# Fourier-layer kernel: column-tiled forward transforms, squares with the channel innermost, a new order on four engines, and the weights' sign on ScalarE

## The chip, the cores and the metric

The kernel runs on one core of a Trainium2 chip. The metric is the device time of one execution in microseconds (us); lower is better. Five compute queues matter: TensorE (PE in the rows, with its weight loads as PEld), VectorE (DVE), ScalarE (ACT), GpSimd (POOL) and SyncE (SP), which only issues transfers.

## The reference, cut to what matters

64 images of 64x64 pixels go through a Fourier neural operator with 32 channels and 4 layers; its tokens, and 77 text tokens, then go through one attention block and one layer of experts.

```python
def spectral_conv(x, w1, w2):                       # x: image, channel, 64, 64
    x_ft = jnp.fft.rfft2(x)
    out_ft[:, :, :M1, :M2]  = einsum('bixy,ioxy->boxy', x_ft[:, :, :M1, :M2], w1)   # M1 = M2 = 12
    out_ft[:, :, -M1:, :M2] = einsum('bixy,ioxy->boxy', x_ft[:, :, -M1:, :M2], w2)
    return jnp.fft.irfft2(out_ft)
h = layer_norm(x @ fc0_w + fc0_b)                   # over the 32 channels
for i in range(4):
    h = layer_norm(spectral_conv(h) + conv_w[i] @ h + conv_b[i])
    if i < 3: h = gelu(h)
h = gelu(h @ fc1) ; h = gelu(h @ fc2) ; h = h @ fc3
```

All numbers are fp32.

## The kernel before, in words

**Passes.** Images are taken in 32 pairs (`PAIRS`). A first pass (the stem) computes the first layer norm in closed form and the forward transform of each pair. Three layer passes follow (`layer(s)`, s = 1, 2, 3), each over the 32 pairs, then a last pass with the three dense layers, then attention and experts. Between passes `mix(s)` multiplies the modes of all images by the layer's weights. The change lies almost wholly in the three layer passes, at about 277 to 765, 800 to 1280 and 1316 to 1800 us.

**One step of a layer pass** handles pair g and finishes pairs g-1 and g-2. A pair is worked in halves h (0, 1) of 1024 values per partition, and each half in units u (0, 1) of 128x512. On TensorE the operations of a step are:

- `widen` (line 527): the inverse transform along x, 512 columns, into the bank that becomes the layer's output; `conv` (line 544) adds the 1x1 convolution on top of it and releases the bank to ScalarE.
- `i1` (line 555): the inverse transform along y for the next pair, 64 products of 32 columns, read out by `z_copy` on ScalarE and VectorE.
- `turn` (line 591): four transposes of the pair before into the single bank `t_mid`, which `hc_copy` (ScalarE, line 929) must empty before the next `turn` may write it. Four `turn`s a step.
- `f1` (line 615): the forward transform along x of the pair before. Per step 128 products, each with 128x32 weights taken from the activations `hp` and 48 moving columns `d1`, in four groups of 32 products; each goes to one of four column tiles 32 wide. A channel takes two products per column tile pair (`a`), and each writes real and imaginary parts interleaved. `a_copy` (ScalarE, line 945) empties the single bank `a_ps` after each group.
- `f2` (line 629): the forward transform along y of pair g-2, two groups of 12 products with 128x64 weights from `asb` and 24 moving columns, on two column tiles 64 wide; `x_copy` reads it out.

An fp32 product is two records in the profile, so a group of 32 products shows as x64; a transpose is one.

**The layer norm** goes round four engines for each unit: `square` (ScalarE, line 903) writes the squares to `sq`, `reduce` (VectorE, line 1238) sums 33 numbers per pixel, `rstds` (POOL, line 1481) takes the power -0.5, `normalise`, `gain` and `bias` (VectorE, lines 1252, 1309, 1316) apply it, and `gelu` (ScalarE, line 915) writes `hp`. `sq` stands as [channel, pixel], 33 x 16, so a pixel's numbers are 16 apart. A bank is used again by `widen` once `normalise` has read it.

**Weights.** Every second step SyncE loads one chunk of the next layer's weights (`load_w`), `w_sum` (VectorE, line 1346) sums it, and `w_centre` (POOL, lines 1491 to 1497) subtracts the mean and multiplies one half by the signs `sgn`; `load_w` of the next chunk waits for that.

**Order.** Nothing is scheduled by a program: each engine runs its queue in the order in which the functions are called, and waits by semaphores. SyncE's queue in a step is `load_w` (every second step), `load_h` for half 0, `store_h` of pair g-2 half 1, `store_h` of pair g-1 half 0 (after both of its `hc_copy`), `load_h` for half 1, and six loads of `gin`, the coefficients of pair g+2, which ScalarE's `coefficients` (lines 967, 969) put in order.

## Time and profile before

| | |
|---|---|
| median of 3 runs | 3216.27 us (3214.8 to 3220.66) |
| profiled execution | 3222.97 us, of which the span is 3221.1 us |
| mean granted TensorE clock | 0.965 of full speed |
| busy share of the span | TensorE 90%, VectorE 69%, ScalarE 67%, POOL 65% |

The rows below come from the profiled execution. Busy shares are means over passes with different limits, so the layer passes are read by themselves. A group's duration reaches a little into the next group of the same engine, so the advance from one group to the next is the difference of their starts.

### The profile page before, as it was taken

To read this page: it belongs to the slowest core of one execution; us is meant where nothing else is said; L and a number is where in the kernel's file an instruction comes from. 1 tells how busy PE (TensorE), PEld (TensorE's weight loads), DVE (VectorE), ACT (ScalarE), POOL (GpSimd) and SP (SyncE) were. 2 spreads that over 40 slices of the span, in tenths; PEclk is the share of its full clock that TensorE was granted. 3 is DMA by queue.
4 is the path that set the end of the run, shared out by engine and by line. 5 is a ranking of instruction groups with operands and counts; after the bars stand their busy time and mean duration, and the time that the engine had idled before them with its cause. 6 is when DMAs were issued, how large, how long until landed. Compare 5 with 4: busy or idle time off the path is not lost. (4 is left out here: it accounts for less than half of the span.)

```text
span 3221.1 us, 190782 instructions
## 1 busy us (share of the span) xinstructions
PE 2893.1 (90%) x80542; PEld 1961.7 (61%) x80542; DVE 2215.7 (69%) x3767; ACT 2148.5 (67%) x3644; POOL 2102.1 (65%) x1147
## 2 busy tenths in 40 slices
PE   6777999997999999699999689999999987999997
PEld 4555777775677777477777534444444424666665
DVE  7765889884888887488898444444444436777775
ACT  4663777774677776477777257777777764666654
POOL 3763899993899997499999344445445434666664
PEclk9997999998899999899999889999999998999998
DMA  5764555554455554455555411111211103111111
GB/s 164 229 224 142 172 173 176 181 172 142 148 176 179 171 181 143 146 175 174 177 175 179 137 52 53 58 55 58 58 55 58 58 21 79 31 30 30 30 30 24
DMA packets 236925, 379.78 MB, mean 118 GB/s; under 512 B 117090, under 2 KB 154786, under 8 KB 236530
## 3 DMA queue, kind: packets, MB, share of 16 engines
q1 hardware_dynamic: 225122, 363.94, 36.7%
q10 hardware_dynamic: 7920, 10.03, 1.0%
q0 software_dynamic: 3744, 3.84, 0.8%
q8 instruction: 101, 1.65, 0.2%
q14 instruction: 38, 0.31, 0.0%
HBM read 217.88 MB, written 159.83 MB: 117 GB/s over the span
## 5 line engine op out<-in xcount | busy, mean ns | idle before, releaser
L1481 POOL TENSOR_TENSOR rstd<-var,mhalf 128x16 f32<-128x16 f32 x512 | 1524.3, 2993 | 694.3 <-DVE var L1238 688.8
L1238 DVE TENSOR_REDUCE var<-sq 128x16 f32<-128x528 f32 x384 | 403.3, 1051 | 93.0 <-ACT sq L903 93.0
L1252 DVE TENSOR_TENSOR zt<-ps,rstd 128x512 f32<-128x512 f32 x512 | 345.1, 684 | 77.8 <-POOL rstd L1481 71.4
L615 PEld LDWEIGHTS ps<-d,hp 128*32 128x32 f32 x24576 | 292.0, 111 | 132.2 <-ACT hp L915 97.3
L615 PE MATMUL ps<-d,hp 128*32 128x48 f32 x24576 | 345.0, 209 | 27.2 <-ACT hp L915 15.2
L544 PEld LDWEIGHTS ps<-cwl,hc 64*64 64x64 f32 x16384 | 272.3, 139 | 139.6 <-issue 133.5
L527 PE MATMUL ps<-zb,ex 48*128 48x512 f32 x1024 | 305.0, 672 | 51.2 <-DVE zt L1252 20.5
L555 PEld LDWEIGHTS ps<-dyi,gt 64*48 64x48 f32 x16384 | 230.1, 124 | 164.2 <-issue 152.5
L1074 ACT ACTIVATE a<-ps,fc1b 128x1024 f32<-128x1024 f32 x256 | 271.1, 1110 | 64.8 <-PE ps L818 64.8
L544 PE MATMUL ps<-cwl,hc 64*64 64x64 f32 x16384 | 308.2, 226 | 0.0
L903 ACT ACTIVATE sq<-ps 128x512 f32<-128x512 f32 x384 | 218.9, 598 | 132.9 <-PE ps L544 123.8
L555 PE MATMUL ps<-dyi,gt 64*48 64x32 f32 x16384 | 272.4, 210 | 36.5 <-ACT gt L969 16.5
L945 ACT COPY asb<-ps 128x384 f32<-128x384 f32 x384 | 191.2, 498 | 169.5 <-PE ps L615 169.5
L1238 DVE TENSOR_REDUCE var<-sql 128x16 f32<-128x528 f32 x128 | 141.6, 1108 | 208.1 <-ACT sql L903 208.1
L915 ACT ACTIVATE hp<-zt 128x512 f32<-128x512 f32 x384 | 231.8, 627 | 78.9 <-DVE zt L1316 78.9
L1309 DVE TENSOR_TENSOR zt<-zt,gbx 128x512 f32<-128x512 f32 x384 | 275.4, 717 | 10.2
L591 PE MATMUL ps<-ident,hp 128*128 128x128 f32 x1536 | 275.5, 303 | 6.3 <-ACT ho L929 4.3
L1316 DVE TENSOR_TENSOR zt<-zt,gbx 128x512 f32<-128x512 f32 x384 | 264.7, 689 | 10.3
L834 PE MATMUL ps<-a,fc 128*64 128x512 f32 x1024 | 253.8, 616 | 3.5 <-ACT a L1074 3.5
L2136 POOL TENSOR_TENSOR sm<-sm,mx 128x952 f32<-128x952 f32 x96 | 170.5, 1776 | 94.7 <-DVE mx L2047 94.7
L929 ACT COPY ho<-ps 128x512 f32<-128x512 f32 x384 | 223.2, 581 | 13.1 <-PE ps L591 5.1
L591 PEld LDWEIGHTS ps<-ident,hp 128*128 128x128 f32 x1536 | 203.5, 197 | 28.9 <-ACT ho L929 7.8
(199 smaller groups left out, 4800.6 us busy)
## 6 DMA issues: line engine op xcount, KB each, us to landing
h_scratch<-ho SPq DMA_DIRECT2D x256, 512.0 KB
hc<-h_scratch SPq DMA_DIRECT2D x256, 512.0 KB, 4.2
wsb<-in_w SPq DMA_DIRECT2D x64, 288.0 KB
gin<-g_scratch SPq DMA_DIRECT2D x252, 72.0 KB
gin<-g_scratch SPq DMA_DIRECT2D x504, 36.0 KB
wc<-expert_scratch SPq DMA_DIRECT2D x64, 129.0 KB, 2.7
g_scratch<-hp ACTq DMA_DIRECT2D x32, 192.0 KB, 4.5
g_scratch<-hp SPq DMA_DIRECT2D x32, 192.0 KB, 4.1
```

The source lines that it names most:

```text
L527: nc.tensor.matmul(main_ps(s, h, u), ex[k], zb[b][k, h, :], start=True, stop=False, skip_group_check=True, tile_position=(64 * u, 0))
L544: last = nc.tensor.matmul(main_ps(s, h, u)[64 * m:64 * m + 64, r:512:8], hc[b][k, 8 * h + r, 64 * m:64 * m + 64], cwl[k], start=False, sto ...
L555: last = nc.tensor.matmul(z[c][64 * u:64 * u + 2 * TRIG, 32 * col:32 * col + 32], gt[b][rows, k].rearrange("k n s a -> k (n s a)"), dyi[ro ...
L591: last = nc.tensor.transpose(t_mid[:, 128 * a:128 * a + 128], src, ident[:])
L615: last = nc.tensor.matmul(a_ps[row:row + 32, 2 * TRIG * k:2 * TRIG * k + 2 * TRIG], hp[b][:, u, 8 * j + k].rearrange("p v r -> p (v r)"), ...
L834: last = nc.tensor.matmul(f2_ps[64 * v:64 * v + 64, u, :], fc2[:], a1[:, 2 * u + v, :], start=True, stop=True, tile_position=(0, 64 * v))
L1074: nc.scalar.activation(a1[:, 2 * u:2 * u + 2, :], f1_ps[:, 2 * u:2 * u + 2, :], ACT.Gelu, bias=fc1b[:]).then_inc(a1_ready, 1)
L1238: nc.vector.tensor_reduce(dst, src, axis=AX.X, op=ALU.add).then_inc(var_ready, 1)
L1252: nc.vector.tensor_tensor(by_px(zt[h][:, u]), by_px(main_ps(s, h, u)), scale, ALU.mult).then_inc(norm_ready, 1)
L1309: nc.vector.tensor_tensor(z, z, channels(s, 0).unsqueeze(2).to_broadcast([128, C, 16]), ALU.mult).then_inc(gain_ready, 1)
L1316: nc.vector.tensor_tensor(z, z, channels(s, 1).unsqueeze(2).to_broadcast([128, C, 16]), ALU.add).then_inc(zt_ready, 1)
L1481: nc.gpsimd.tensor_tensor(rstd[u][:], var[u][:], mhalf[:], ALU.pow).then_inc(rstd_ready, 1)
```

## The change

- **`f1`** takes each half of the trigonometric matrix by itself: a product now has 24 moving columns (`dx`) in place of 48, one column tile pair holds the real and one the imaginary parts, and one group covers 16 channels (64 products) in place of 8, with the same 128 products per step. `a_copy` then runs twice a step in place of four times, as a plain copy of 128x384. `asb` is one buffer [channel, x mode] in place of two.
- **`f2`** uses four column tiles 32 wide: 24 products per group in place of 12, with 128x32 weights that are read 24 elements apart, and `dy` as moving operand.
- **`square`** reads its bank 16 elements apart and writes `sq` as [pixel, channel], so `reduce` reads contiguously.
- **The sign** of the weights is applied by ScalarE (`w_sign`, in the odd half step of every second pair) in place of POOL, except in the first pass; `w_centre` moves between two powers of the second pair, and `w_sum` from the end to the start of the first pair's step.
- **Orders**: TensorE runs `conv`, `i1` in one piece, `f1`, `turn`, `f1` where `f1` and `i1` alternated; ScalarE's and VectorE's queues are reordered; SyncE's queue is as before. Weights and constants are laid out for this, and two constants more are loaded.

```diff
             def f1(s, b, g, j):
...
-                pe.wait_ge(a_ready, 4 * rank(s, g) + j)
-                for k in range(8):
-                    for a in range(2):
+                pe.wait_ge(a_ready, 2 * rank(s, g) + j)
+                for k in range(CH):
+                    for part in range(2):
                         for u in range(2):
-                            row = 64 * a + 32 * u
-                            last = nc.tensor.matmul(a_ps[row:row + 32, 2 * TRIG * k:2 * TRIG * k + 2 * TRIG],
-                                                    hp[b][:, u, 8 * j + k].rearrange("p v r -> p (v r)"),
-                                                    d1[:, a].rearrange("p x s -> p (x s)"),
+                            row = 64 * part + 32 * u
+                            last = nc.tensor.matmul(a_ps[row:row + 32, 2 * KX * k:2 * KX * k + 2 * KX],
+                                                    hp[b][:, u, CH * j + k].rearrange("p v r -> p (v r)"), dx[:, part],
                                                     start=True, stop=True, tile_position=(0, row))
...
                 for a in range(6):
                     for c in range(2):
-                        o = KY * (6 * m + a)
-                        last = nc.tensor.matmul(x_ps[64 * c:64 * c + 64, o:o + KY],
-                                                asb[b][:, KX * m + 2 * a + c].rearrange("y c s -> y (c s)"),
-                                                cy[:], start=True, stop=True, tile_position=(0, 64 * c))
+                        for part in range(2):
+                            o, row = KY * (6 * m + a), 64 * c + 32 * part
+                            last = nc.tensor.matmul(x_ps[row:row + 32, o:o + KY], asb[:, :, KX * m + 2 * a + c],
+                                                    dy[:, part], start=True, stop=True, tile_position=(0, row))
...
                     if here:
                         widen(s, 0, g, 1)
+                        conv(s, 0, g, 1)
+                        with where_next(g):
+                            i1(s, g + 1, 0, CH)
                     if old:
                         f1(s, 0, g - 1, 0)
-                    if here:
-                        conv(s, 0, g, 1)
-                    for j, piece in enumerate(((0, 6), (6, 11), (11, 16))):
...
+                    if old:
+                        turn(s, 0, g - 1, 1, 0)
+                        f1(s, 0, g - 1, 1)
...
-                    dst = sq[u][:, 0:C, :].rearrange("p (v c) n -> p v (c n)", v=2)
...
+                    dst = sq[u][:, :, 0:C]
+                by_px = (lambda tile: tile.rearrange("p (v n) -> p v n", v=2)) if is_last(s) else (
+                    lambda tile: tile.rearrange("p (c n) -> p n c", c=C))
+                nc.scalar.activation(dst, by_px(main_ps(s, h, u)), ACT.Square).then_inc(sq_ready, 1)
...
-                nc.scalar.copy(asb[b][:, :, 8 * j:8 * j + 8, :].rearrange("p x g s -> p g x s"),
-                               a_ps.rearrange("p (g x s) -> p g x s", g=8, s=2)).then_inc(a_ready, 1)
+            def a_copy(s, g, j):
+
+                act.wait_ge(a_psr, 2 * rank(s, g) + j + 1)
+                nc.scalar.copy(asb[:, CH * j:CH * j + CH].rearrange("p c x -> p (c x)"), a_ps).then_inc(a_ready, 1)
...
+            def w_sign(s, i):
+
+                k = COUPLES * s + i
+                first = wsb[:, bass.ds(i * WCH, WCH), 0, :]
+                act.wait_ge(w_sub, 2 * k + 2)
+                nc.scalar.activation(first, first, ACT.Copy, scale=sgn[:]).then_inc(w_cent, 1)
...
                 def odd(i, p):
                     here, old, nxt = (where(i, p, 0, lag) for lag in (0, 2, -2))
-                    if old:
-                        a_copy(s, 0, old[0], 0)
                     if here:
                         square(s, here[0], 1, 0)
+                    if old:
+                        hc_copy(s, old[0], 0, 1)
+                        a_copy(s, old[0], 0)
+                    if here:
                         square(s, here[0], 1, 1)
-                    if old:
-                        a_copy(s, 0, old[0], 1)
-                        a_copy(s, 0, old[0], 2)
                     if nxt:
                         z_copy(s, nxt[0])
                     if old:
                         hc_copy(s, old[0], 1, 0)
-                        a_copy(s, 0, old[0], 3)
+                        a_copy(s, old[0], 1)
+                    if here and p == 1:
+                        w_sign(s, i)
...
                 else:
-                    dst, src = var[u][:], sq[u][:].rearrange("p c n -> p n c")
+                    dst, src = var[u][:], sq[u][:]
                 nc.vector.tensor_reduce(dst, src, axis=AX.X, op=ALU.add).then_inc(var_ready, 1)
...
                                         ALU.subtract).then_inc(w_sub, 1)
+                if s is not STEM:
+                    return
...
                         for u in range(2):
                             rstds(s, 2 * i + p, h, u)
-                        if p == 0 and h == 1 and not final:
-                            w_centre(s, i)
+                            if p == 1 and h == 0 and u == 0 and not final:
+                                w_centre(s, i)
```

TensorE's queue before, in the middle of a layer step, from `widen` of half 1 on (`d` is `d1`; x counts products):

```order
L527 MATMUL ps<-zb,ex 128x512 x2
L608 REGISTER_ALU
L615 MATMUL ps<-d,hp 32x48 x32
L544 MATMUL ps<-cwl,hc 64x64 x32
L722 COMPARE_AND_BRANCH
L563 ISA
L565 REGISTER_ALU
L555 MATMUL ps<-dyi,gt 48x32 x24
L757 UNCONDITIONAL_BRANCH
L615 MATMUL ps<-d,hp 32x48 x32
L722 COMPARE_AND_BRANCH
L555 MATMUL ps<-dyi,gt 48x32 x20
```

The same stretch of TensorE's queue after the change:

```order
L521 ISA
L530 MATMUL ps<-zb,ex 128x512 x2
L547 MATMUL ps<-cwl,hc 64x64 x32
L724 COMPARE_AND_BRANCH
L566 ISA
L568 REGISTER_ALU
L558 MATMUL ps<-dyi,gt 48x32 x64
L754 UNCONDITIONAL_BRANCH
L611 REGISTER_ALU
L613 REGISTER_ALU
L618 MATMUL ps<-dx,hp 32x24 x64
L594 MATMUL ps<-ident,hp 128x128 x4
```

The first `f1` group no longer stands between `widen` and `conv`, `i1` is one group of 64 products ahead of `f1`, and `turn` (line 594 now) stands between the two `f1` groups.

ScalarE's queue before, from `hc_copy` of half 0 (`ho0`) to the first `a_copy` (`asb0`), with buffer numbers:

```order
L929 COPY ho0<-ps 128x512
L964 ISA
L967 COPY gt0<-gin 128x64x6
L914 REGISTER_ALU
L915 ACTIVATE hp0<-zt1 128x64x8
L922 REGISTER_ALU
L929 COPY ho0<-ps 128x512
L954 REGISTER_ALU
L959 ISA
L959 COPY xsb<-ps 128x144x2
L969 ACTIVATE gt0<-gin,side 128x64x6
L945 COPY asb0<-ps 128x8x24x2
```

ScalarE's queue after the change, from the last `gelu` of the even half step through the odd one:

```order
L914 ACTIVATE hp0<-zt1 128x64x8
L894 REGISTER_ALU
L48 ISA
L903 ACTIVATE sq0<-ps 128x16x32
L921 REGISTER_ALU
L928 COPY ho0<-ps 128x512
L944 COPY asb<-ps 128x384
L903 ACTIVATE sq1<-ps 128x16x32
L948 COPY zb0<-ps 112x16x2x16
L921 REGISTER_ALU
L928 COPY ho1<-ps 128x512
L944 COPY asb<-ps 128x384
```

The second `hc_copy` of half 0 has moved behind the first square of half 1 (`sq0`), and the second square (`sq1`) now stands behind `a_copy`, which waits for an `f1` group of 64 products.

POOL's queue before, from the last power of the first pair of two:

```order
L1481 TENSOR_TENSOR rstd<-var,mhalf 128x16
L1489 ISA
L1491 TENSOR_SCALAR wmean<-wmean 128x18
L1492 ISA
L1493 ISA
L1493 TENSOR_TENSOR wsb<-wsb,wmean 128x576
L1495 REGISTER_ALU
L1497 TENSOR_TENSOR wsb<-wsb,sgn 128x9x32
L1479 ISA
L1481 TENSOR_TENSOR rstd<-var,mhalf 128x16
```

POOL's queue after the change, from the first power of the second pair:

```order
L1490 TENSOR_TENSOR rstd<-var,mhalf 128x16
L1498 ISA
L1500 TENSOR_SCALAR wmean<-wmean 128x18
L1501 ISA
L1502 ISA
L1502 TENSOR_TENSOR wsb<-wsb,wmean 128x576
L1488 REGISTER_ALU
L1490 TENSOR_TENSOR rstd<-var,mhalf 128x16
```

The multiplication by `sgn` has left POOL's queue (it is ScalarE's `w_sign` now), and the other two instructions stand one power later.

## Rows read from the trace of the kernel before

**Rows 1.** Busy time by engine in 380 us in the middle of the second layer.
```profile
880.00:1260.00 380.00, 367.17 (x15290) 292.00 (x15286) 340.11 (x461) 285.69 (x527) 345.49 (x148) 1.00 0.56 174
```

**Rows 2.** TensorE's timeline, second layer: start, duration, group, records, [idle before].
```profile
1000.57 0.89 PE L615 MATMUL ps<-d,hp 128*32 128x48 f32 x64 [0.31 <-ACT hp L915]
...
1007.96 1.13 PE L527 MATMUL ps<-zb,ex 48*128 48x512 f32 x4 [0.25 <-DVE zb L1321]
...
1010.13 0.71 PE L591 MATMUL ps<-ident,hp 128*128 128x128 f32 x4
1010.77 0.89 PE L629 MATMUL ps<-cy,asb 128*64 128x24 f32 x24
1011.61 0.69 PE L591 MATMUL ps<-ident,hp 128*128 128x128 f32 x4
...
1016.89 0.74 PE L555 MATMUL ps<-dyi,gt 64*48 64x32 f32 x48
1017.56 0.89 PE L615 MATMUL ps<-d,hp 128*32 128x48 f32 x64
1018.38 0.65 PE L555 MATMUL ps<-dyi,gt 64*48 64x32 f32 x40
```

**Rows 3.** POOL's timeline over two image pairs, second layer.
```profile
1005.22 6.04 POOL L1481 TENSOR_TENSOR rstd<-var,mhalf 128x16 f32<-128x16 f32 x2 [0.43 <-DVE var L1238]
...
1024.89 0.27 POOL L1491 TENSOR_SCALAR wmean<-wmean 128x18 f32<-128x18 f32 x1
1025.37 1.16 POOL L1493 TENSOR_TENSOR wsb<-wsb,wmean 128x576 f32 x1 [0.20 <-POOL wmean L1491]
1026.72 0.67 POOL L1497 TENSOR_TENSOR wsb<-wsb,sgn 128x288 f32 x1 [0.19 <-POOL wsb L1493]
...
1034.03 6.03 POOL L1481 TENSOR_TENSOR rstd<-var,mhalf 128x16 f32<-128x16 f32 x2 [0.43 <-DVE var L1238]
```

**Rows 4.** TensorE's timeline in the first pass: the small transform `f2_x`.
```profile
156.77 0.66 PE L678 MATMUL ps<-cy,hp 128*8 128x24 f32 x48
157.35 0.49 PE L512 MATMUL ps<-quad,xin 128*128 128x128 f32 x2
```

**Rows 5.** Groups by line: busy us, mean ns of one, idle before.
```profile
L1238 DVE TENSOR_REDUCE var<-sq 128x16 f32<-128x528 f32 x384 | 403.3, 1051 | 93.0 <-ACT sq L903 93.0
L903 ACT ACTIVATE sq<-ps 128x512 f32<-128x512 f32 x384 | 218.9, 598 | 132.9 <-PE ps L544 123.8
L959 ACT COPY xsb<-ps 128x288 f32 (+1 forms) x96 | 41.4, 432 | 2.8 <-PE ps L629 2.8
L1346 DVE TENSOR_REDUCE wmean<-wsb 128x18 f32 (+1 forms) x64 | 47.8, 748 | 12.3 <-DMA wsb<-in_w 12.2
L1058 ACT COPY hp<-ps 128x384 f32<-128x384 f32 x32 | 15.1, 478 | 28.5 <-PE ps L797 21.2 <-issue 3.6 <-DVE hp L1442 1.6
```

**Rows 6.** ScalarE's timeline: the copy of the transposed half.
```profile
1014.72 0.57 ACT L929 COPY ho<-ps 128x512 f32<-128x512 f32 x1
```

**Rows 7.** SyncE's DMA issues in one step of the second layer.
```profile
1011.71 4.16 SPq L379 DMA_DIRECT2D h_scratch<-ho  x2
1017.12 0.35 SPq L382 DMA_DIRECT2D hc<-h_scratch  x1
...
1019.81 0.72 SPq L308 DMA_DIRECT2D gin<-g_scratch  x2
```

**Rows 8.** ScalarE and its queue before the second layer: rows loaded, then read.
```profile
790.35 0.85 ACTq L308 DMA_DIRECT2D gin<-g_scratch  x2
793.43 0.83 ACT L967 COPY gt<-gin 128x384 f32<-128x384 f32 x1 [9.41 <-DMA gin<-g_scratch]
```

**Rows 9.** First pass: one weight chunk's load, and the sum that reads it.
```profile
107.53 0.37 SPq L369 DMA_DIRECT2D wsb<-in_w  x1
...
111.88 0.75 DVE L1346 TENSOR_REDUCE wmean<-wsb 128x18 f32 x1 [0.73 <-DMA wsb<-in_w]
```

More of the change, by code:

```diff
@@ L109, in token_network @@
         gt = [sb(f"gt{p}", [128, CH, 4, 2, KX // 2]) for p in range(2)]
-        asb = [sb(f"asb{p}", [128, 2 * KX, C, 2]) for p in range(2)]
-        sq = [sb(f"sq{u}", [128, C + 1, 16]) for u in range(2)]
+        asb = sb("asb", [128, C, 2 * KX])
+        grow = sb("grow", [128, 2 * 768])
+        sq = [sb(f"sq{u}", [128, 16, C + 1]) for u in range(2)]
         sql = [sb(f"sql{u}", [128, 2, C + 1, 8]) for u in range(2)]
@@ L1017, in even @@
                         hc_copy(s, older[0], 1, 1)
-                    if here:
-                        square(s, here[0], 0, 1)
-                    if old:
-                        gelu(s, old[0], 1, 0)
-                        hc_copy(s, old[0], 0, 0)
                     if here and nxt:
@@ L1377, in even @@
                     if old:
+                        gain(s, *old, 0)
+                        bias(s, *old, 0)
                         normalise(s, *old, 1)
+                    if here and p == 0:
+                        w_sum(s, i)
+                    if old:
                         gain(s, *old, 1)
-                        bias(s, *old, 1)
                     if here:
                         reduce(s, *here, 1)
+                    if old:
+                        bias(s, *old, 1)
                 def odd(i, p):
@@ L1388, in odd @@
                         gain(s, *old, 0)
-                        bias(s, *old, 0)
                     if here:
                         reduce(s, *here, 0)
+                    if old:
+                        bias(s, *old, 0)
+                    if nxt := where(i, p, 0, -2):
+                        z_copy(s, nxt[0])
                     if old:
@@ L1397, in odd @@
                         gain(s, *old, 1)
-                    if nxt := where(i, p, 0, -2):
-                        z_copy(s, nxt[0])
-                    if old:
                         bias(s, *old, 1)
-                    if here and p == 0:
-                        w_sum(s, i)
                 each_step(dve, lambda i, p, h: odd(i, p) if h else even(i, p), 2, 2)
@@ L2271, in layouts @@
     out["d1"] = d1.reshape(128, 2, TRIG, 2)
+    out["dx"] = d1[:, :, 0].reshape(128, TRIG, 2).transpose(0, 2, 1)
     ex = ex.reshape(2, KX // 2, 2, 2, 128).transpose(0, 2, 3, 1, 4).reshape(2 * TRIG, 128)
```

75 lines of the change are left out of this document (35 added, 40 removed).

## Prediction

> **What bounds the kernel now.** I read the busy time of each engine by stretches first. In the middle of a layer pass TensorE is busy 367 of 380 us (97%), POOL 345 (91%), VectorE 340 (90%), ScalarE 286 (75%), at full clock [rows 1]. So the layer passes hang on TensorE, with POOL and VectorE close behind, and an edit that relieves one of the three alone stops at the next. POOL's timeline gives the length of a step: the same power starts at 1005.22 and at 1034.03 us, two pairs later, so a step takes 14.41 us [rows 3]; 96 steps are 1383 us. Of these 14.41, POOL's four powers take 2 x 6.04 = 12.08, its work on the weights (0.27 + 0.20 + 1.16 + 0.19 + 0.67 = 2.49 every second step) 1.25, and the rest, 1.08, is waiting for VectorE's sums, 0.43 of it in each row shown [rows 3].
>
> TensorE's timeline shows groups without gaps but two: 0.25 before `widen`, which waits for `z_copy`, and 0.31 before the first `f1` group, for `gelu` [rows 2]. A gap like the first stands in every step, one like the second in about every other.
>
> **`f1` and `i1`.** A group of 64 `f1` records advances the queue by 0.82 (1017.56 to 1018.38), or 12.8 ns each. `i1` with 48 records advances by 0.67, one with 40 (0.65 less the overlap of 0.07) by 0.58: so a record costs 11 ns and a group 0.13 of its own [rows 2]. Moving columns halve in `f1`, records stay 256 per step. The nearest row for 24 columns on four column tiles is the stem's `f2_x`: 48 records in 0.58 (156.77 to 157.35) [rows 4], hardly less each than 48 columns cost. Less 0.13 that is 9.4 ns, so a group of 128 takes 128 x 9.4 + 130 = 1.33 us at the least, 1.55 at a full 12.1 ns, and 1.64 if nothing is gained. I take 1.40, since the groups are long: 2 x (1.64 - 1.40) = 0.48 saved per step. `i1` in one piece: 128 x 11 + 130 = 1.54, against 0.67 + 0.58 + 0.58 = 1.83 for three; I take 1.60, 0.23 saved.
>
> **`f2`.** A group advances by 0.84 now (1010.77 to 1011.61), 35 ns for each of 24 records [rows 2]. The new one has 48 records of the shape of [rows 4], so 0.58; the weights read 24 elements apart may cost more. But little of this 0.26 arrives. Three `turn`s stand round the two `f2` groups and share one bank: 0.71 for the transposes [rows 2], 0.57 for ScalarE's copy [rows 6] and two hand-overs of about 0.07 make 1.42 from one `turn` to the next, against 0.64 + 0.84 = 1.48 now. Saved: 2 x 0.06 = 0.12, and TensorE gets two new gaps of 0.2. By the same rule `f2` may cost 0.78 without losing anything of the sum.
>
> **Gaps.** `i1` ends about 3.4 us before `widen` (two `f1` groups and a `turn` follow it) and no longer one `f1` group before, so the 0.25 goes; `f1` now stands behind `conv` and `i1`, so the half of 0.31 goes too. The second `f1` group waits for `a_copy`: 0.48 [rows 5] and the hand-overs against a `turn` of 0.64 between; 0.05. TensorE's step: 14.41 - 0.48 - 0.23 - 0.12 - 0.25 - 0.15 + 0.05 = 13.23.
>
> **Sums and sign.** `reduce` takes 1051 ns for 528 numbers that it reads 16 apart, `w_sum` 748 for 576 side by side [rows 5]; 748 x 528 / 576 = 686, with its fixed part some 700. Four times 0.35 is 1.4 us of VectorE's step, which falls from 12.9 to 11.5. The Trainium skill (SBUF — State Buffer, the note on cachelines in "Door 1: The DMA port swizzle") says that SBUF is read in lines of 16 bytes and that each new line costs; the two rows agree. POOL loses the sign, 0.67 + 0.19, less one hand-over: 2.49 becomes about 1.73, its step without waits 12.08 + 0.87 = 12.95. ScalarE takes the sign: nearest is `x_copy`, 288 numbers in 432 ns [rows 5], 0.25 per step with a factor read beside; it loses two of four `a_copy`, 1.0. It has 25% to spare. So TensorE still sets the step, 0.3 above POOL.
>
> **Squares.** ScalarE now reads the bank 64 bytes apart; no row has that shape. `x_copy` reads 144 elements apart: 432 ns for 288, where 384 contiguous take 478 and 512 take 598 [rows 5], so about 400 by their slope: 30 ns lost. The other bound is VectorE's loss in SBUF, 1051 - 700 over 528 numbers, which gives 340 ns for a square. I take 0.05 per square (0.63 to 0.65), since the reader and the memory are those of `x_copy`, and ScalarE's room hides most of it.
>
> **Moved waits.** The second square of half 1 stands behind `a_copy`, hence behind `i1` and 64 products of `f1`: 1.6 + 1.4 + 0.5 after `conv`. POOL has the power of unit 0 (3.02) meanwhile, begun some 1.4 after `conv`, and is free at 4.4 to 4.5; the second sum is there at about 3.5 + 0.6 + 0.7 + 0.2 = 5.0 if POOL runs close behind. This may cost 0.5 in POOL, which has 13.23 - 12.95 = 0.3 to give and runs behind mostly.
>
> SyncE's queue is unchanged but waits elsewhere. `store_h` of half 0 waits for the `hc_copy` that moved behind a square of half 1, and `load_h` and all six `gin` loads are queued behind it. Now the store is issued well before `load_h` (1011.71 + 4.16 against 1017.12), and the last `gin` load begins 3.05 us after `load_h` (1019.81 + 0.36) [rows 7]. After: `conv` end + 0.1 + 0.5 + 0.6 + 0.1 for square and copy (up to 0.6 more behind `gelu`) + 0.7 for the store + 3.05 = 5.1 to 5.7. `coefficients` of the next step wants them 1.3 after the next first `conv`: 1.6 + 1.4 + 0.64 + 1.4 + 1.06 + 1.12 + 1.3 = 8.5. So 2.8 to 3.4 us are left to land. Alone, the last load (issued at about 790.8) was read at 793.43, 2.6 us later [rows 8]; a chunk of 288 KB in the busy first pass took 4.35 (107.53 to 111.88) [rows 9]. I take 0.1 per step.
>
> The weights: `w_sign` ends about 1.15 before the end of `conv` of half 0, `w_sum` starts 3.4 after it, so the chunk has 4.5 us against 4.35 [rows 9]. Whatever is late falls on VectorE every second step, with `gain` and `reduce` behind it; 0 to 0.25, taken 0.05.
>
> **Sum.** 13.23 + 0.17 = 13.4 us a step; (14.41 - 13.4) x 96 = 97 us less. Two more constants are loaded at the start and three small VectorE instructions added: +2. The profiled execution took 3222.97 us, 6.7 above the median of the runs, so 3128 in its terms and **3121 us** as a median. Its own range, 13.2 to 13.6 a step, is 3102 to 3140.
>
> **The rivals.**
> - *TensorE gains more* (0.15). If an `f1` record falls with its columns, to 6.4 ns, its groups take 0.95 and POOL becomes the bound at 12.95 and a small wait, 13.05: 131 us less, 3087. For it: both `i1` (32 columns, 11 ns) and `f1` (48, 12.8) cost in the order of their columns. Against: 24 columns at 12.1 [rows 4].
> - *Strided squares* (0.10). With 340 ns more per square the chain from `conv` to the power is longer by that in each half: 13.75, 3155. The Trainium skill (PSUM — Partial Sum Buffer, Specifications) gives PSUM lines of 8 bytes and warns of non-contiguous access for matmuls; for ScalarE's reads `x_copy` speaks against it.
> - *The loads are late* (0.10). If `gin` takes 4.35 to land, ScalarE stands in front of `coefficients` for 1 us or more, with the `hc_copy` behind it that `turn` needs, and the step grows until the load fits: about 13.95, 3174.
> - *Slower* (0.05). `f2` costs 35 ns per record now, `f1` 12.8 with twice the columns. If that price belongs to the record and its source and not to weights 64 wide on two tiles, 48 records take 1.68, the turn chain hides nothing, and the step is 13.35 + 2 x 0.84 = 15.0: 60 us more, 3278. It decides from 1.37 us a group, 28 ns a record. The Trainium skill (TensorE: Matmul & The Clock Gate, "Wait — 56ns, not 53.3ns?") speaks for this side: starts never come closer than about 25 ns however few the columns. By that 96 records would be 2.4 us a step in place of 1.2. The trace disagrees already, with 12.1 and 12.8 ns per record on four tiles [rows 2, 4].
> - *Within 0.2%* (0.03): several of these together.
>
> **How the numbers follow.** A measurement tells about 0.2%, 6 us. My forecast has 0.57. The three other faster cases end between 3087 and 3174; leaving out a little at their ends and the last two gives 3085 to 3172 for 8 in 10. Faster by over 0.2%: 0.57 + 0.15 + 0.10 + 0.10 = 0.92; within: 0.03; slower: 0.05.
>
> **What would show it.** Two steps of POOL at 26.8 in place of 28.8 us; `f1` groups of 128 records advancing by 1.40 and `f2` by 0.58, with a gap before the second and third `turn` for the `hc_copy`; no gap before `widen` of half 0; `reduce` at 0.70; squares at 0.63; POOL's waits down to 0.4 a step; `coefficients` rarely waiting for a transfer. I am wrong if a square takes over 0.8, if `coefficients` or `w_sum` wait for DMA in most steps, or if `f1`'s group is below 1.2 or above 1.6.

## The result, and the profile after

The changed kernel takes 3179.16 us (median of 4 runs, 3172.68 to 3184.09), against 3217.68 for the kernel before on the same chip: ratio 0.988, interval 0.986 to 0.990. That is 38.5 us less; 97 were forecast. It is faster, as forecast, but the time lies 7 us above the top of the range. The profiled execution took 3178.70 us. Of all executions of the runs below one, of e9, was in a slower state of the chip (4144 us at a mean granted clock of 0.55, the others of e9 about 3171) and is left out.

First the busy time in 360 us in the middle of the second layer (columns as in [rows 1]: stretch, TensorE, its weight loads, VectorE, ScalarE, POOL, clock, DMA share, GB/s):

```profile
880.00:1240.00 360.00, 339.34 (x16233) 275.30 (x16226) 297.97 (x454) 258.79 (x477) 342.08 (x131) 1.00 0.59 178
```

TensorE is down from 97 to 94%, VectorE from 90 to 83, ScalarE from 75 to 72. POOL is up from 91 to 95%. No engine is full, so something else sets the step. TensorE's timeline (start, duration, group, records, [idle before]) answers to [rows 2]:

```profile
1000.91 1.16 PE L547 MATMUL ps<-cwl,hc 64*64 64x64 f32 x64
...
1002.67 0.97 PE L632 MATMUL ps<-dy,asb 128*32 128x24 f32 x48
1003.57 0.72 PE L594 MATMUL ps<-ident,hp 128*128 128x128 f32 x4
...
1005.49 0.71 PE L594 MATMUL ps<-ident,hp 128*128 128x128 f32 x4 [0.29 <-ACT ho L928]
...
1008.40 1.64 PE L558 MATMUL ps<-dyi,gt 64*48 64x32 f32 x128
1009.97 1.28 PE L618 MATMUL ps<-dx,hp 128*32 128x24 f32 x128
1011.18 0.72 PE L594 MATMUL ps<-ident,hp 128*128 128x128 f32 x4
...
1013.67 1.13 PE L530 MATMUL ps<-zb,ex 48*128 48x512 f32 x4 [0.31 <-issue]
...
1019.97 0.71 PE L594 MATMUL ps<-ident,hp 128*128 128x128 f32 x4 [0.95 <-ACT ho L928]
...
1028.95 1.16 PE L547 MATMUL ps<-cwl,hc 64*64 64x64 f32 x64
```

These two steps take 28.04 us, from 1000.91 to 1028.95, so each of them takes 14.02 in place of 14.41. But the steps of this kernel come out unequal, mostly 13.2 to 14.5 us each, and two of them don't give the mean. POOL's division of a weights' mean stands once in every second step, and the two rows below are 26 steps apart:

```profile
869.02 0.56 POOL L1500 TENSOR_SCALAR wmean<-wmean 128x18 f32<-128x18 f32 x1
...
1230.47 0.56 POOL L1500 TENSOR_SCALAR wmean<-wmean 128x18 f32<-128x18 f32 x1
```

That is 361.45 / 26 = 13.90 in the second layer; the same reading gives 13.86 and 13.87 in the other two, so a step takes **13.88** on average. In the kernel before it gives 14.41 in all three. Of 0.53 x 96 = 51 us, 38.5 arrive as a gain of the whole; the rest is taken up in the last part.

In the rows above, `i1` advances the queue by 1.57 (1008.40 to 1009.97), `f1` by 1.21, `f2` by 0.90. The third `turn` of each step waits for `ho`, that is for `hc_copy`: 0.29 in one step, 0.95 in the next, 0.62 on average. ScalarE's timeline says why that copy is late:

```profile
1002.77 0.59 ACT L928 COPY ho<-ps 128x512 f32<-128x512 f32 x1
1004.05 0.90 ACT L965 COPY gt<-gin 128x384 f32<-128x384 f32 x1 [0.68 <-DMA gin<-g_scratch]
1004.86 0.58 ACT L928 COPY ho<-ps 128x512 f32<-128x512 f32 x1
...
1016.59 0.59 ACT L928 COPY ho<-ps 128x512 f32<-128x512 f32 x1
1018.57 0.86 ACT L965 COPY gt<-gin 128x384 f32<-128x384 f32 x1 [1.39 <-DMA gin<-g_scratch]
```

`coefficients` (L965) stands ahead of it and waits for a transfer. By the list of waits it does so 86 times, for 90.6 us in all; before, the same wait was 26.1 us in 3 places, at the starts of the layers. The loads it waits for are late on SyncE, whose issues answer to [rows 7]:

```profile
1000.07 0.33 SPq L311 DMA_DIRECT2D gin<-g_scratch  x1
...
1003.63 6.63 SPq L382 DMA_DIRECT2D h_scratch<-ho  x2
1010.60 0.35 SPq L385 DMA_DIRECT2D hc<-h_scratch  x1
...
1013.38 0.72 SPq L311 DMA_DIRECT2D gin<-g_scratch  x2
```

The second store of the pair waits for the moved `hc_copy`, which ends at 1009.57, and `load_h` and the six `gin` loads come behind it. `coefficients` waits for all six. The last `gin` load begins at 1013.38 + 0.36 = 1013.74 and is read at 1018.57, 4.8 us later; in the step before, 1000.07 to 1004.05, it was 4.0.

POOL, as in [rows 3], is second:

```profile
1003.72 3.28 POOL L1490 TENSOR_TENSOR rstd<-var,mhalf 128x16 f32<-128x16 f32 x1 [0.80 <-DVE var L1245]
1007.08 0.56 POOL L1500 TENSOR_SCALAR wmean<-wmean 128x18 f32<-128x18 f32 x1
1007.86 1.16 POOL L1502 TENSOR_TENSOR wsb<-wsb,wmean 128x576 f32 x1 [0.22 <-POOL wmean L1500]
1008.97 11.98 POOL L1490 TENSOR_TENSOR rstd<-var,mhalf 128x16 f32<-128x16 f32 x4
```

A single power shown here takes 3.28 us (two took 6.04 before, [rows 3]); `wmean` takes 0.56 in place of 0.27. Last, from the groups by line over the whole run, as in [rows 5], VectorE's sum; it is at the forecast 0.70.

```profile
L1245 DVE TENSOR_REDUCE var<-sq 128x16 f32<-128x528 f32 x384 | 267.9, 698 | 189.5 <-ACT sq L903 173.8
```

Two theories for the missing 0.5 us a step (13.88 in place of 13.4; 0.6 in the two steps shown) follow. **Loads:** the store waits for the moved copy, `gin` lands late, `coefficients` holds up `hc_copy`, and through `turn` and `widen` the delay runs round to the next store. **POOL:** powers and weights, some 13.3 us a step, hold it.

### The profile page after: what moved, and what is told of

It reads as the page before. It is cut to its first block and busy times, and to the rows that moved or that the text cites. A ratio compares the mean times of both kernels' runs of the same rounds, so it can differ in the third digit from the quotient of the medians.

```text
span 3176.9 us, 199484 instructions
## 1 busy us (share of the span) xinstructions
PE 2820.0 (89%) x85132; PEld 1925.4 (61%) x85132; DVE 2086.8 (66%) x3770; ACT 2075.8 (65%) x3500; POOL 2115.6 (67%) x1099
## 5 line engine op out<-in xcount | busy, mean ns | idle before, releaser
L1490 POOL TENSOR_TENSOR rstd<-var,mhalf 128x16 f32<-128x16 f32 x512 | 1554.9, 3057 | 643.9 <-DVE var L1245 643.1
L1245 DVE TENSOR_REDUCE var<-sq 128x16 f32<-128x528 f32 x384 | 267.9, 698 | 189.5 <-ACT sq L903 173.8
L594 PE MATMUL ps<-ident,hp 128*128 128x128 f32 x1536 | 277.1, 304 | 46.7 <-ACT ho L928 41.5
L558 PEld LDWEIGHTS ps<-dyi,gt 64*48 64x48 f32 x16384 | 215.7, 125 | 140.4 <-issue 140.3
L1316 DVE TENSOR_TENSOR zt<-zt,gbx 128x512 f32<-128x512 f32 x384 | 296.5, 772 | 5.6
L618 PE MATMUL ps<-dx,hp 128*32 128x24 f32 x24576 | 271.9, 193 | 31.4 <-issue 29.0
L903 ACT ACTIVATE sq<-ps 128x512 f32<-128x512 f32 x384 | 230.1, 600 | 87.9 <-PE ps L547 86.0
L618 PEld LDWEIGHTS ps<-dx,hp 128*32 128x32 f32 x24576 | 249.7, 110 | 53.2 <-issue 37.8
L914 ACT ACTIVATE hp<-zt 128x512 f32<-128x512 f32 x384 | 240.3, 629 | 59.0 <-DVE zt L1323 53.4
L1323 DVE TENSOR_TENSOR zt<-zt,gbx 128x512 f32<-128x512 f32 x384 | 264.9, 690 | 6.8
L558 PE MATMUL ps<-dyi,gt 64*48 64x32 f32 x16384 | 237.3, 210 | 29.6 <-ACT gt L967 15.9
L944 ACT COPY asb<-ps 128x384 f32<-128x384 f32 x192 | 92.0, 479 | 212.7 <-PE ps L618 212.6
```

What stands on the lines that cost most here:

```text
L558: last = nc.tensor.matmul(z[c][64 * u:64 * u + 2 * TRIG, 32 * col:32 * col + 32], gt[b][rows, k].rearrange("k n s a -> k (n s a)"), dyi[ro ...
L594: last = nc.tensor.transpose(t_mid[:, 128 * a:128 * a + 128], src, ident[:])
L618: last = nc.tensor.matmul(a_ps[row:row + 32, 2 * KX * k:2 * KX * k + 2 * KX], hp[b][:, u, CH * j + k].rearrange("p v r -> p (v r)"), dx[:, ...
L1245: nc.vector.tensor_reduce(dst, src, axis=AX.X, op=ALU.add).then_inc(var_ready, 1)
L1316: nc.vector.tensor_tensor(z, z, channels(s, 0).unsqueeze(2).to_broadcast([128, C, 16]), ALU.mult).then_inc(gain_ready, 1)
L1323: nc.vector.tensor_tensor(z, z, channels(s, 1).unsqueeze(2).to_broadcast([128, C, 16]), ALU.add).then_inc(zt_ready, 1)
```

## The experiments

All times are medians; the ratio is to the kernel before, timed beside each. "After" is the changed kernel. The step is read from rows shown here, or, marked ~, a mean over steps that come out unequal or whose rows are not shown (for the changed kernel that of the three layer passes above).

| kernel | us | ratio (95%) | step |
|---|---|---|---|
| after | 3179 | 0.988 (0.986 to 0.990) | ~13.9 |
| e1: after, store behind the loads | 3131 | 0.973 (0.971 to 0.974) | 13.38 |
| e2: after, half of the powers | 3230 | 1.003 (0.999 to 1.007) | uneven |
| e3: e1 and e2 | 3105 | 0.964 (0.963 to 0.966) | 13.16 |
| e4: after, sign on POOL | 3192 | 0.991 (0.989 to 0.993) | ~14.0 |
| e5: e1, means on VectorE | 3116 | 0.969 (0.968 to 0.971) | 13.18 |
| e6: after, `hc_copy` moved back | 3146 | 0.977 (0.976 to 0.979) | ~13.5 |
| e7: before, store behind the loads | 3219 | 1.001 (1.000 to 1.002) | ~14.4 |
| e8: e1, sign on POOL | 3155 | 0.981 (0.979 to 0.982) | ~13.7 |
| e9: e1, squares strided again | 3171 | 0.985 (0.983 to 0.987) | ~13.8 |
| e10: e3, `f2` weights side by side, copy writes strided | 3119 | 0.970 (0.968 to 0.972) | ~13.4 |
| e11: e1, `gain` short | 3116 | 0.969 (0.967 to 0.971) | ~13.2 |
| e12: e5, `f2` weights as in e10 | 3134 | 0.973 (0.972 to 0.975) | ~13.4 |
| e13: e5, `f2` weights side by side, copy reads strided | **3104** | 0.965 (0.963 to 0.966) | 13.02 |
| e14: e3, `f2` weights as in e13 | 3094 | 0.963 (0.961 to 0.964) | 13.02 |
| e15: after, `coefficients` later | 3144 | 0.978 (0.977 to 0.980) | ~13.5 |

### e1 to e4: loads or POOL

e1, in SyncE's `layer_pass`:

```diff
-                    if h == 0:
-                        for lag in (3, 2):
-                            if c := where(i, p, h, lag):
-                                store_h(s, *c)
+                    if c := where(i, p, h, 3):
+                        store_h(s, *c)
```

> The changed kernel (3179 us, 14.02 us a step), with one edit: in a layer pass SyncE's store of the older row, half 0, which waits for ScalarE's copy in the odd half step, is queued behind the loads of the odd half step and no longer ahead of them. Loads theory: what holds the step at 14.02 and not at 13.4 is that the six loads of gin are issued late (from 1011.3 on, where they could go some 5 us sooner), so that coefficients waits for them 0.7 to 1.4 us in 86 of 96 steps. Then the wait of L965 for a transfer falls from 90 us to under 20, a step takes 13.4 to 13.6, and the time is 3121 to 3140. POOL theory: the step is held by POOL's powers, 3.11 us each beside VectorE, and its weights (13.3 of 14.02 us busy). Then the waits of coefficients go and the step stays within 0.1 of 14.02: 3170 to 3180.

Measured: 3131 us. SyncE's timeline, ScalarE's and POOL's, in that order:

```profile
1011.07 0.33 SPq L385 DMA_DIRECT2D hc<-h_scratch  x1
...
1013.71 0.72 SPq L311 DMA_DIRECT2D gin<-g_scratch  x2
1014.77 0.38 SPq L382 DMA_DIRECT2D h_scratch<-ho  x1
```
```profile
1005.96 0.89 ACT L963 COPY gt<-gin 128x384 f32<-128x384 f32 x1
```
```profile
1006.43 3.28 POOL L1488 TENSOR_TENSOR rstd<-var,mhalf 128x16 f32<-128x16 f32 x1 [0.17 <-DVE var L1243]
...
1033.18 3.27 POOL L1488 TENSOR_TENSOR rstd<-var,mhalf 128x16 f32<-128x16 f32 x1 [0.18 <-DVE var L1243]
```

`coefficients` no longer waits in any step (27.3 us in 3 places are left, the layers' starts). Two steps take 1033.18 - 1006.43 = 26.75, the 26.8 that the prediction named as its sign. The loads theory holds: the place of one store in SyncE's queue is worth 48 us. The edit does two things at once, which it doesn't separate: the last `gin` load is issued 3.4 us after the end of `conv` (1010.70 to 1014.07) in place of 5.4, and the store of half 0 no longer runs ahead of it. POOL is now 98% busy, so it is next.

e2, POOL's power, in the layer passes and the last pass (a constant is set once in the rest):

```diff
-  nc.gpsimd.tensor_tensor(rstd[u][:], var[u][:], mhalf[:], ALU.pow)
+  nc.gpsimd.tensor_tensor(rstd[u][:, 0:8], var[u][:, 0:8], mhalf[:, 0:8], ALU.pow)
```

> The changed kernel, with the powers of the layer passes over 8 of the 16 columns: it leaves out half of the reciprocal deviations (a constant stands there in their place), so POOL's four powers of a step take about half, and POOL's step is some 7.5 us in place of 13.3. POOL theory: the step falls to TensorE's 13.2 to 13.5, 3110 to 3140. Loads theory: coefficients goes on waiting for its transfer in most steps and the time stays at 3165 to 3180.

Measured: 3230 us, *slower* than the changed kernel by 51. POOL is not the bound of the changed kernel, but neither theory had this. TensorE's timeline and the busy times of 5 us in it show part of why:

```profile
436.75 0.97 PE L632 MATMUL ps<-dy,asb 128*32 128x24 f32 x48
439.55 1.12 PE L594 MATMUL ps<-ident,hp 128*128 128x128 f32 x4 [1.83 <-ACT ho L928]
440.60 2.08 PE L530 MATMUL ps<-zb,ex 48*128 48x512 f32 x4
```
```profile
440.00:445.00 5.00, 5.00 (x104) 3.17 (x106) 2.66 (x5) 2.43 (x5) 2.01 (x1) 0.50 0.08 34
```

With POOL quick the step still runs into the late load: `coefficients` waited 2.29 us there, and `turn` 1.83 behind it. Round that idle stretch TensorE's granted clock fell to 0.50 of full, 1.2 in place of 2.4 GHz; `widen` took 2.08 where it takes 1.13 (as again at 450.02). It doesn't do so each time:

```profile
532.37 0.71 PE L594 MATMUL ps<-ident,hp 128*128 128x128 f32 x4 [2.06 <-ACT ho L928]
```

After this longer wait the clock stayed at full (1.00 over 530 to 540 us), and `widen` took 1.13. In the changed kernel the wait of 0.95 in the first rows left the clock at full, but behind one of 1.35, at 1076.16, `conv` took 1.98 where it takes 1.16, at 0.50 over 1078 to 1081 us. So in e2 steps of 13.2 us stand beside steps of 14 to 18. Over the whole run `coefficients` waits 121.5 us for its load in place of 90.6, and TensorE's `turn` 64.8 for the copy in place of 41.5; how the 51 us divide between these waits and the clock, and why the waits are longer with a quicker POOL, no run shows.

e3 joins both edits.

> Both edits together: the store behind the loads and half of the powers left out. If each of the two alone moves little because the other holds the step right behind it, this one alone falls to TensorE's own work, 12.9 to 13.3 a step, 3075 to 3115. Loads theory alone: as with the store behind the loads alone, 3121 to 3140. POOL theory alone: as with half of the powers alone, 3110 to 3140.

Measured: 3105 us. Two of POOL's rows, two steps apart, and 300 us of the first layer pass:

```profile
1009.24 2.01 POOL L1491 TENSOR_TENSOR rstd<-var,mhalf 128x8 f32<-128x8 f32 x1 [2.11 <-DVE var L1243]
...
1035.56 2.02 POOL L1491 TENSOR_TENSOR rstd<-var,mhalf 128x8 f32<-128x8 f32 x1 [2.10 <-DVE var L1243]
```
```profile
370.00:670.00 300.00, 292.77 (x14438) 237.50 (x14440) 261.63 (x399) 224.99 (x421) 203.56 (x114) 1.00 0.61 193
```

A step is (1035.56 - 1009.24) / 2 = 13.16, at full clock, with TensorE 98% busy. The late load holds the step at 13.9, POOL right behind it at 13.38, TensorE at 13.16.

e4 gives POOL the sign back (and takes `w_sign` from ScalarE).

```diff
-                if s is not STEM:
-                    return
...
-                    if here and p == 1:
-                        w_sign(s, i)
```

> The changed kernel with one part undone: POOL multiplies the weights by their signs again in the layer passes (0.67 us and 0.19 of hand-over in every second step), ScalarE's w_sign is gone (0.54). POOL theory: 0.43 a step more, 3215 to 3225. Loads theory: POOL has 0.7 us a step to spare, and ScalarE has less to do ahead of the loads' waits: 3170 to 3190.

Measured: 3192 us, 13 more; just above the loads theory's range and far from POOL's.

### e6, e7, e15: which part of the change made the loads late

e6 puts `hc_copy(s, old[0], 0, 1)` back to the end of ScalarE's even half step.

```diff
                         gelu(s, old[0], 1, 1)
+                        hc_copy(s, old[0], 0, 1)
...
                     if old:
-                        hc_copy(s, old[0], 0, 1)
                         a_copy(s, old[0], 0)
```

> The changed kernel with one of its moved steps undone and nothing else: ScalarE's copy of half 0, unit 1 stands at the end of the even half step again, ahead of the squares of half 1. If the moved copy is what makes the store late, and the store the loads behind it, then SyncE's wait ahead of load_h and gin shortens by some 2 us or more, coefficients waits in few steps, and the time comes near that with the store behind the loads: 3128 to 3150. If the store is late for another reason, 3170 to 3182.

e15 leaves that copy late and moves both `coefficients` behind the copy of unit 0 and the second square.

```diff
-                        coefficients(s, nxt[0], 0)
-                    if old:
                         hc_copy(s, old[0], 0, 0)
                     if here:
                         square(s, here[0], 0, 1)
                     if here and nxt:
+                        coefficients(s, nxt[0], 0)
                         coefficients(s, nxt[0], 1)
```

> The changed kernel (3179 us) with one move of ScalarE's order undone in part: coefficients stands behind the hc_copy of half 0 and the second square, not ahead of them; the store stays ahead of the loads and as late. If a late gin costs time because hc_copy, and behind it TensorE's turn, stand in its queue, the wait gets some 1.1 us of cover, nearly all of it is gone, and the time is 3130 to 3150. If the late loads cost by another way (i1, or the loads behind them), 3165 to 3182.

e7 makes the edit of e1 on the kernel before.

> The kernel before (3218 us, 14.41 us a step, TensorE 97% busy), with the same edit of SyncE's queue as alone: the store of half 0 behind the loads of the odd half step. If the late loads are a thing that the change made, there is nothing to gain here: 3210 to 3224. If the order of the queue cost time before the change already, 14.0 a step and 3180.

Measured: e6 3146 us, e15 3144, e7 3219. Each of the two moves undone alone returns 33 to 36 of the 48 us, and the kernel before has nothing to gain from SyncE's order. So most of the loss needs both moves: the copy that makes the store late, and `coefficients` ahead of the `hc_copy` that `turn` wants. In e15 the wait of `coefficients` is down to 26.5 us in 3 places, though the store is as late as ever: it starts 4.7 us after the last load is issued (1010.17 to 1014.89), since an `hc_copy`, a square and a wait of 0.96 for `turn` now stand in front of it. In e6 the wait is still there 66 times, 55.2 us in all. What keeps each of the two 12 to 15 us above e1 was not looked into. e7 has the narrower meaning: before the change TensorE was 97% busy and `coefficients` waited at the starts of the layers alone.

### e5, e8, e11: POOL behind the loads

e5 divides the weights' means on VectorE, behind its sum, in place of POOL.

```diff
                                         axis=AX.X, op=ALU.add).then_inc(w_mean, 1)
+                dve.wait_ge(w_mean, 2 * (COUPLES * s + i) + 1)
+                nc.vector.tensor_scalar(wmean[:], wmean[:], 1.0 / C, None, ALU.mult).then_inc(w_mean, 1)
...
-                nc.gpsimd.tensor_scalar(wmean[:], wmean[:], 1.0 / C, None, ALU.mult).then_inc(w_sub, 1)
```

> The kernel with the store behind the loads (3131 us, 13.38 us a step, POOL 98% busy), and the division of the weights' means (0.56 us and 0.22 of hand-over on POOL in every second step) done by VectorE behind its sum. If POOL holds the step there, its work falls by 0.39 to 12.99 and TensorE's 13.16 is next: 13.2 a step, 17 us less, 3110 to 3120. If TensorE or a chain through it holds 13.38 already, nothing: 3126 to 3136.

Measured: 3116 us, as expected. TensorE's timeline has no wait left but the one ahead of `widen`, put down to "issue", and 1002.97 to 1016.15, 13.18, is its own step (POOL is busy 298.0 of the 300 us from 880 on, so both bounds are reached here):

```profile
1002.97 1.13 PE L528 MATMUL ps<-zb,ex 48*128 48x512 f32 x4 [0.26 <-issue]
...
1005.14 0.71 PE L592 MATMUL ps<-ident,hp 128*128 128x128 f32 x4
1005.78 0.97 PE L630 MATMUL ps<-dy,asb 128*32 128x24 f32 x48
1006.69 0.71 PE L592 MATMUL ps<-ident,hp 128*128 128x128 f32 x4
...
1016.15 1.13 PE L528 MATMUL ps<-zb,ex 48*128 48x512 f32 x4 [0.28 <-issue]
```

e8 is e1 with the sign on POOL as in e4.

> The kernel with the store behind the loads, and the sign back on POOL. With the loads out of the way POOL holds the step at 13.38, so that its 0.67 to 0.88 and 0.19 in every second step should now count in full, 0.43 to 0.53 a step: 13.8 to 13.9, 3172 to 3182. If POOL did not hold the step, 3131 to 3140. The changed kernel itself lost 13 us by the same edit.

e11 is e1 with `gain` over one channel of 32 in the layer passes (the rest stays unscaled).

```diff
-  nc.vector.tensor_tensor(z, z, channels(s, 0).unsqueeze(2).to_broadcast([128, C, 16]), ALU.mult)
+  nc.vector.tensor_tensor(z[:, 0:1], z[:, 0:1], channels(s, 0)[:, 0:1].unsqueeze(2).to_broadcast([128, 1, 16]), ALU.mult)
```

> The kernel with the store behind the loads (3131 us; powers of 3.10 us, POOL bound at 13.38), with gain multiplying one channel of 32 in the layer passes: it leaves out most of the scaling, and VectorE has 0.7 us less to do in each of four places of a step. If POOL's powers take 3.10 and not 2.99 because VectorE reads two operands beside them, they fall to 3.0 or less, POOL's step to 12.9 or 13.0, and TensorE's 13.16 is left: 3110 to 3118. If the powers take what they take whatever VectorE does, 3.08 to 3.11 and 3126 to 3134.

Measured: e8 3155 us, 24 more than e1, as by POOL's bound, but half of what I expected; e11 3116 us. POOL's groups over 880 to 1180 us of e1, e8 and e11, in that order (busy us, mean ns):

```profile
L1488 POOL TENSOR_TENSOR rstd<-var,mhalf 128x16 f32<-128x16 f32 x91 | 279.6, 3096 | 1.8 <-DVE var L1243 1.8
```
```profile
L1486 POOL TENSOR_TENSOR rstd<-var,mhalf 128x16 f32<-128x16 f32 x88 | 265.5, 3039 | 1.8 <-DVE var L1241 1.8
```
```profile
L1492 POOL TENSOR_TENSOR rstd<-var,mhalf 128x16 f32<-128x16 f32 x92 | 275.6, 3020 | 7.3 <-DVE var L1243 7.3
L1502 POOL TENSOR_SCALAR wmean<-wmean 128x18 f32<-128x18 f32 x11 | 3.0, 276 | 0.9
```

The power has no fixed price: 3.10 us in e1, 3.04 where the sign shifts it against VectorE's work, 3.02 with `gain` gone, and `wmean` falls back to 0.28. That accounts for e8: sign and hand-over, (0.88 + 0.19) / 2 = 0.53 a step, less 4 x 0.057 = 0.23 from shorter powers, is 0.30, or 29 us, against 24 measured. The Trainium skill (SBUF — State Buffer, "Who interferes with whom") says that VectorE's second port to SBUF is also GpSimd's only one and is held by one of them at a time; e11 agrees in direction. Which of VectorE's instructions meets which power I did not separate.

### e9: the squares' layout

e9 is e1 with the squares written channel by channel again, as before the change.

```diff
-        sq = [sb(f"sq{u}", [128, 16, C + 1]) for u in range(2)]
+        sq = [sb(f"sq{u}", [128, C + 1, 16]) for u in range(2)]
```

> The kernel with the store behind the loads (3131 us, 13.38 us a step), with the squares written channel by channel again, so that the reduction reads them 16 apart (1051 in place of 697 ns, four in a step). VectorE's step grows by 1.4, from about 11.5 to 12.9, and each sum comes to POOL 0.35 later. If POOL's own work holds the step and the sums come well ahead of it, next to nothing is lost: 3131 to 3140. If sum and power follow each other closely (POOL waits 2.0 us in 360 for a sum now, and 26 before the change), 0.3 to 0.5 a step: 3160 to 3180.

Measured: 3171 us, 40 more than e1: in 200 us from 900 on VectorE is busy 183.8 in place of 171.7, and POOL waits for sums 12.7 us in 300 in place of 1.8. The layout is worth some 0.4 a step once the loads are out of the way, though VectorE is full in neither (92 and 86%).

### e10, e12, e13, e14: the price of `f2`

`f2` reads 32 weights 96 bytes apart. Four kernels store `asb` so that they lie side by side; the copy then either writes (e10, e12) or reads (e13, e14) out of order.

```diff
-        asb = sb("asb", [128, C, 2 * KX])
+        asb = sb("asb", [128, 2 * KX, C])
...
-  asb[:, :, KX * m + 2 * a + c],
+  asb[:, KX * m + 2 * a + c, :],
```

The copy in e10 and e12, and then in e13 and e14:

```diff
+  nc.scalar.copy(asb[:, :, CH * j:CH * j + CH].rearrange("p x c -> p c x"), a_ps.rearrange("p (c x) -> p c x", c=CH))
```
```diff
+  nc.scalar.copy(asb[:, :, CH * j:CH * j + CH], a_ps.rearrange("p (c x) -> p x c", c=CH))
```

> The kernel with the store behind the loads and half of the powers left out (3105 us, 13.16 us a step, TensorE 97.5% busy), with asb stored so that the 32 weights of each f2 record lie side by side and not 96 bytes apart; ScalarE's a_copy writes them 128 bytes apart instead. If the stride is what makes a group of 48 records advance by 0.90 in place of the 0.58 of the stem's, two groups give 0.64 back: 12.5 a step, 61 us less, 3044 (3040 to 3060). If the price of a record is another thing (48 records at 18.6 ns whatever the stride), 3100 to 3108. The mean of an a_copy shows what its writing costs (0.48 now).

> A version to beat both kernels, the whole reference computed: the store behind the loads, the means divided by VectorE, and asb with the 32 weights of an f2 record side by side. TensorE's step falls to some 12.5 if the stride costs 0.64, and POOL's 12.99 to 13.1 holds it: 3100 to 3110. If the stride costs nothing, as with the means on VectorE: 3112 to 3120.

> As the version with everything (store behind the loads, means on VectorE, f2's weights side by side), but ScalarE's a_copy goes through the bank 96 bytes apart and writes 16 channels in a row, where that version read in order and wrote single numbers 128 bytes apart (0.82 us). If the price of the copy came from its writes, it falls back to 0.48 to 0.55, TensorE's step to 12.6, and POOL's 13.0 to 13.1 holds it: 3098 to 3108. If it came from the change of order as such, 0.8 and 3130 to 3138 again.

> The store behind the loads, half of the powers left out (a constant stands for them), f2's weights side by side, the copy reading strided. With POOL out of the way TensorE's step shows what f2's stride costs: 12.5 to 12.7 in place of 13.16, 3045 to 3065, if the copy is at 0.48 to 0.55; 13.36 and 3119 again if it is at 0.8.

Measured: e10 3119 us, 14 *more* than e3; e12 3134, 18 more than e5; e13 3104; e14 3094. ScalarE's copy in e12 and in e13 (880 to 1180 us):

```profile
L942 ACT COPY asb<-ps 128x384 f32<-128x384 f32 x44 | 36.1, 820 | 28.5 <-PE ps L616 28.5
```
```profile
L942 ACT COPY asb<-ps 128x384 f32<-128x384 f32 x47 | 22.5, 479 | 29.8 <-PE ps L616 29.8
```

Single numbers written 128 bytes apart cost 0.34 us a copy; the same reordering done while reading the bank, with 16 numbers written in a row, costs nothing. TensorE's timeline of e14:

```profile
1011.91 1.13 PE L528 MATMUL ps<-zb,ex 48*128 48x512 f32 x4 [0.26 <-issue]
...
1014.08 0.71 PE L592 MATMUL ps<-ident,hp 128*128 128x128 f32 x4
1014.73 0.62 PE L630 MATMUL ps<-dy,asb 128*32 128x24 f32 x48
1015.56 0.69 PE L592 MATMUL ps<-ident,hp 128*128 128x128 f32 x4 [0.22 <-ACT ho L926]
...
1016.92 0.72 PE L592 MATMUL ps<-ident,hp 128*128 128x128 f32 x4
...
1024.93 1.13 PE L528 MATMUL ps<-zb,ex 48*128 48x512 f32 x4 [0.27 <-issue]
```

An `f2` group lasts 0.62 in place of 0.97 (0.66 in [rows 4]), so the stride is what its records cost. Yet the step falls only from 13.16 to 13.02 (1011.91 to 1024.93), and I expected 12.5 to 12.7. A `turn` comes 1.48 and 1.36 behind the one before, 1.42 on average, because it waits for `hc_copy`: the very chain that the prediction worked out, and that my expectation for these runs forgot. By that chain alone the step would be 13.16 - 2 x (1.55 - 1.42) = 12.90. The other 0.12 lies behind the third `turn`, after which the next `widen` starts 0.76 later (1017.68) and in e3 0.65; what holds it no row shows. e13 computes the whole reference and is the fastest kernel that does, 113 us below the kernel before. TensorE's timeline of it, one step:

```profile
1000.34 1.13 PE L528 MATMUL ps<-zb,ex 48*128 48x512 f32 x4 [0.28 <-DVE zt L1257]
...
1013.36 1.13 PE L528 MATMUL ps<-zb,ex 48*128 48x512 f32 x4 [0.26 <-issue]
```

That is 13.02 too. One such wait in two is now for VectorE, which stands behind POOL, and POOL idles 0.1 us in 300 ahead of its powers. So both bounds are reached in this kernel: POOL is full, and e14, with half of the powers, takes the same 13.02.

## Why the prediction was off

**The step that failed** is "I take 0.1 per step", for the `gin` loads. Everything up to it was right: the store waits for the moved copy, the loads queue behind it, they are issued 5.1 to 5.7 us after the end of `conv` (1008.35, from a row not shown, to 1013.74 is 5.4), and 2.8 to 3.4 are left for them to land (1013.74 to the end of the copy ahead of `coefficients`, 1017.18, is 3.4). What was wrong is the landing time. I had 2.6 for a load alone [rows 8] and 4.35 behind much traffic [rows 9], and chose by the first, though these loads follow a store and a load of half a pair (512 KB each). The trace has 4.0 and 4.8 from issue to use, and the late load cost some 0.5 a step. With 4.35 the prediction had the rest too, as the rival "the loads are late": `coefficients` in front of `hc_copy`, `turn` late, 13.95 a step, 3174 us. It came to 13.88 and 3179. e1, e6 and e15 show that mechanism, and e1 prices it at 48 us; it had a chance of 0.10.

**The factor of 96** hid the rest. Of the 58 us between 3121 and 3179 the steps hold 0.48 x 96 = 46. The other 12 were mostly lost because a saving per step did not arrive 96 times: the changed kernel saves 0.53 a step, or 51 us, and its median is 38.5 lower; e1 saves 1.05, or 101, and is 88 lower (its mean step, read as above, is 13.36). So 12 to 13 us went outside the steady steps, in the first steps of each pass or outside the passes, where the prediction put 2; which of them no run separates. That is why e1, whose step is no longer than the forecast 13.4, takes 3131 and not 3121. It isn't a fixed sum: e3 and e5 both take 13.17 a step on average and are 11 us apart.

**POOL's step**, 12.95, was too short by 0.43: e1 runs at 13.38. The powers take 3.10 and not 3.02 (4 x 0.08 = 0.3) and the means 0.56 and not 0.27, with 0.22 to hand over (0.15). I took both from the trace of before as if they were fixed; e11 shows that they hang on what VectorE does beside them. That e1 lands at 13.38 beside a forecast of 13.4 is partly luck: the forecast had TensorE at 13.23 and 0.17 for waits, and POOL holds the step. e1's 3131 is inside the likeliest case's own range (3102 to 3140). The feared wait of POOL behind the second square cost 0.17 to 0.18 in every second step, in e1.

**TensorE's step**, forecast at 13.23, is 13.16 in e3, where nothing else holds it, and 13.18 in e5, but three of its terms erred and nearly cancelled. `f1` groups advance by 1.21 and not 1.40: 0.38 better. `f2` advances by 0.90 and not 0.58, above the 0.78 up to which the turn chain would have hidden it: from `turn` to `turn` it is 1.55 (1005.14 to 1006.69) and not 1.42, 0.26 worse. And the gap of 0.25 before `widen` did not go: 0.26 to 0.31 stand there in every kernel whose rows are shown, mostly waiting for nothing that the profile shows. Before, it was put down to `zb`, and I believed it; so a cause named by the semaphore that came last was counted as gained. Together (0.38 less 0.26 and 0.28) the step would be 0.16 us longer than forecast; 0.08 comes back from `i1` (1.57 for 1.60) and a gap for `a_copy` that never opened, and some 0.1 I cannot place. The gap before `f1` is gone as forecast.

**Right as forecast:** the sum at 0.70 in place of 1.05; squares at 0.60 with a stride of 64 bytes in the bank, the same as in order (0.60), so the rival of strided squares was empty; the weights' load, which VectorE waits for once in 360 us, 0.2; and no sign of the slower case, since `f2`'s 18.8 ns per record (0.90 / 48) stays under the 28 that it needed.

## What to carry to other kernels

When a step moves behind another on one engine, follow every queue whose next wait it feeds: here a copy moved by one square made a store late, and seven loads that had nothing to do with it stood behind that store. A load whose time left is near its landing time must be priced at its landing behind the same traffic, and an instruction that may wait for it belongs behind, not ahead of, whatever the busiest engine wants from its engine. And before counting a gain, name the next two bounds: here they stood at 13.9, 13.38 and 13.16 us, so that the quicker POOL of e2 could not show what it was worth until the load was out of the way. Last, a saving in the steady step, times the number of steps, was more than arrived: 12 to 13 us of it were missing in the changed kernel and in e1.

## What the runs showed of the hardware

- Single waits of `turn` in an otherwise busy stream came with TensorE's granted clock at 0.50 behind them: one of 1.83 us (e2, at 439.55) and one of 1.35 (the changed kernel, at 1076.16). Others did not: one of 0.95 (the changed kernel) and even one of 2.06 (e2, at 532.37). A wait can cost twice, but its length alone did not tell when.
- POOL's power over 16 numbers a partition took 3.02 to 3.10 us by what VectorE did beside it, a product over 18 numbers 0.28 or 0.56; over 8 numbers the power took 2.0 (2.03 in e3), so by a straight line through the two, an estimate, about 1.0 of it is fixed.
- ScalarE read a bank 64 bytes apart (squares, 0.60 us before and after) or 96 bytes apart (copy in e13, 0.48 as in order) at no cost, but writing single numbers 128 bytes apart to SBUF took 0.82 us in place of 0.48 for 384.
- On four column tiles, weights 96 bytes apart took a group of 48 records from 0.62 (e14) to 0.97 us (e5).
